# Attention scores of two heads issued in turn, and the expert broadcast, the output stage and the PSUM ring put back to one plain order

## The chip, the cores and the metric

The kernel runs on all 8 cores of one Trainium2 chip. Each core has its own batch entry and all the weights; nothing is exchanged between cores. The metric is the device time in microseconds of the slowest core.

## The reference

For each of 8 batch entries x is 2048 tokens by 1024 features. Attention has 16 heads of 64. The feed-forward part has 8 experts with 4096 hidden features; every token goes to its two best experts, but all experts are computed for all tokens and weighted with `comb`, which is zero elsewhere. Both parts read the same normed input, and both are added to x.

```python
xn = layernorm(x)                        # no scale, no shift
q, k, v = split(xn @ qkv_w.T + qkv_b)    # 16 heads of 64
attn = softmax(q @ k.T / sqrt(64))       # 2048 x 2048 for each head
a = (attn @ v) @ proj_w.T + proj_b
g = xn @ gate_w + gate_b                 # top 2 of 8, softmax over the two
h = gelu(xn @ w1[e] + b1[e])             # for every expert e, 4096 wide
f = sum over e of comb[e] * (h @ w2[e] + b2[e])
out = x + a + f
```

## The kernel before, in words

The program is emitted in one order, and each engine runs its own instructions in that order; a wait at the head of an engine's queue holds all that is behind it. PSUM is four pages `pg0` to `pg3` of 1024 f32 columns, each with two halves of 512. `pread(page, half, token)` notes who read a half last, and `pdeps` makes the next matmul into it wait for that reader. All weights come through two staging buffers `stg` (`stream`, L240): a 512 KB load on the SyncE queue, and a cast to bf16 on VectorE.

**Layernorm** (L290 to L330). 16 tiles of 128 tokens, one after the other: sum on VectorE, mean, squares, variance and root on ScalarE with a reciprocal on VectorE between, the normed tile on VectorE, 8 transposes on TensorE and a copy into `xnT` on ScalarE. Tiles use two sets of small columns and two `xntok` buffers in turn. In the order of emission all steps of a tile stand before those of the next.

**Attention**, for 8 pairs of heads (`hp`; h01 is the head within the pair). `stageA` does two things. `qkv_chunk` makes q and k of both heads, 16 groups of 8 matmuls and a copy on ScalarE each. `p1_chunk` (the max pass) goes over 16 blocks of 128 queries: 8 score matmuls, alternately of the two heads, a row maximum of each on VectorE (L478), then for each head a maximum over four columns (L486), a cast (L491) and a transpose (L502) that puts the negative maximum into row 65 of q, which a copy of 1x1024 on ScalarE places there twice per head. Both draw their PSUM halves from a ring of six, `ASLOTS` (L425).

`stageB` goes over 4 blocks of 512 queries (`qc`), and for each of them first one head, then the other: `p2_chunk` (the score pass of one head) and `av_chunk`. `p2_chunk` issues 16 score matmuls of 512 columns in 8 pairs; a pair fills both halves of one page, and one Exp of 1024 columns on ScalarE reads it. Pages 0 and 1 take turns from pair to pair:

```python
for ktp in range(8):
    page = st["p2n"] % 2
    st["p2n"] += 1
    tks = []
    for j in range(2):
        deps = tmax(aug_tok[b_], attnT_free[h01], pdeps(page, j))
        tks.append(mm(deps, half(page, j)[:, 0:QC], ...))
    ev = act(tks, attnT[h01][...], pg[page][:, :], AF.Exp, scale=1.0 / 8.0)
```

`av_chunk` waits for the last Exp of its head, then makes four groups of 16 small matmuls into page 2 (head 0) or page 3 (head 1), with a reciprocal (L578) and a scaling (L581) on VectorE between two groups of the same page.

**Experts**, 2 token chunks of 1024 by 8 experts, 16 passes. The first half of a pass (the w1 half) is 32 weight blocks x 2 x 8 matmuls of 512 columns with a Gelu on ScalarE each 8; the second (the w2 half) is 8 output blocks `dt` x 2 x 32 matmuls, each 32 followed on VectorE by `ysc` (L797, times the broadcast weight `combbc`) and the addition into `accT` (L802). `cb_emit` (L680) makes `combbc`, two matmuls and two copies on ScalarE; it is called for the next pass after `dt == 2` of this one, into the other of two `combbc` buffers.

**Output.** `emit_final` (L706) is called once after each token chunk, for its 8 tiles: load x into one of three `fxr`, 8 transposes, an addition on VectorE (L723) into one of two `fout`, a store on the GpSimd queue. Its loads wait for the additions into `accT` of their own 512 tokens only.

Of the kernel before, what the change touches and what calls it, by code (L numbers as in the profile page):

```python
# [17 lines left out]
E = 8  # L18
# [11 lines left out]
OPT_A6 = True  # L30
OPT_CB_PRE = True
OPT_FIN_SPLIT = True
OPT_LN2 = True
# [68 lines left out]
def build_program():  # L102
# [48 lines left out]
    cols = nc.alloc_sbuf_tensor("cols", [128, 28], F32)  # L151
# [11 lines left out]
    def at(name, shape, dtype, off):  # L163
# [14 lines left out]
             for i in range(2)]  # L178
# [3 lines left out]
    combbc = [at(f"combbc{i}", [128, 1024], BF16, 90112 + i * 2048)  # L182
              for i in range(2)]
    ysc = [at(f"ysc{i}", [128, 512], BF16, 147456 + i * 1024) for i in range(2)]
    xsq = at("xsq", [128, 1024], F32, 94208)
    xntok = [at(f"xntok{i}", [128, 1024], BF16, 98304 + i * 2048)
             for i in range(2)]
    accT = at("accT", [128, ND * S], BF16, 94208)
    aoutT = at("aoutT", [128, ND * S], BF16, 126976)
    fxr = [at(f"fxr{i}", [128, 1024], F32, 126976 + i * 4096) for i in range(3)]  # L190
    fout = [at(f"fout{i}", [128, 1024], F32, 139264 + i * 4096) for i in range(2)]
# [89 lines left out]
    prev_nm = [None, None]  # L281
    prev_iv = [None, None]
    prev_r = [None, None]
    prev_xn = [None, None]
    prev_tp = [None, None]
    LNC = [(0, 1, 2, 3, 13, 14), (20, 21, 22, 23, 24, 25)]

    xnT_r = xnT[:, :].rearrange("p (d t) -> p d t", d=ND)
    for tt in range(NT):
        pp = (tt % 2) if OPT_LN2 else 0  # L290
        cNS, cNM, cS2, cR, cVA, cIV = (cols[:, j:j + 1] for j in LNC[pp])
        xs = xring[tt % 3]
        xnt = xntok[pp if OPT_LN2 else 0]
        tok_x = dma_in(tmax(xring_free[tt % 3]), xs[:, :],
                       d_x[tt * 128:(tt + 1) * 128, :], sem=f"sX{tt % 3}")
        t_ns = dve(tmax(tok_x, prev_nm[pp]),
                   lambda e, i=xs, o=cNS: e.reduce_sum(o, i[:, :], AX.X,
                                                       negate=True))
        t_nm = act(tmax(t_ns, prev_xn[pp]), cNM, cNS, AF.Identity,
                   scale=1.0 / DM)  # L300
        prev_nm[pp] = t_nm
        t_sq = act([t_nm], xsq[:, :], xs[:, :], AF.Square, bias=cNM,
                   accum=cS2)
        t_va = act(tmax(t_sq, prev_iv[pp], t_consts), cVA, cS2,
                   AF.Identity, scale=1.0 / DM, bias=epscol)
        t_iv = dve(tmax(t_va, prev_r[pp]),
                   lambda e, o=cIV, i=cVA: e.reciprocal(o, i))
        prev_iv[pp] = t_iv
        t_r = act(tmax(t_iv, prev_xn[pp]), cR, cIV, AF.Sqrt)
        prev_r[pp] = t_r  # L310
        t_xn = dve(tmax(t_r, prev_tp[pp]),
                   lambda e, i=xs, o=xnt, m=cNM, r=cR:
                   e.tensor_scalar(o[:, :], i[:, :], m, r, ALU.add, ALU.mult))
        prev_xn[pp] = t_xn
        xring_free[tt % 3] = t_xn
        page = tt % 2
        tp = None
        for dt in range(ND):
            deps = tmax(t_xn, t_id, pdeps(page, 0)) if dt == 0 else []
            tp = tr(deps, pgb[page][:, dt * 128:(dt + 1) * 128],  # L320
                    xnt[:, dt * 128:(dt + 1) * 128], inc=(dt == ND - 1))
        prev_tp[pp] = tp
# [96 lines left out]
    aug_tok = [None] * 4  # L419
    aot_r = [a[:, :].rearrange("p (t c) -> p t c", t=NT) for a in aot]  # L420

    def stageA(hp):
        ring = hp % 2
        chunks = []
        ASLOTS = [(0, 0), (0, 1), (1, 0), (1, 1), (2, 0), (3, 0)]  # L425
        st = {"qk_tok": [], "mq_evs": [[], []], "aqn": 0}

        def qkv_chunk(h01, iq, u, n4):
            def go():
                b_ = 2 * ring + h01  # L430
                buf = qh[b_] if iq == 0 else kh[b_]
                if n4 == 0:
                    st[("w", u)] = stream([wqk_free[u % 3]], wqkbf[u % 3][:, :],
                                          d_wqk[u])
                page, hh = ASLOTS[st["aqn"] % 6]
                st["aqn"] += 1
                deps = tmax(st[("w", u)], ln_all, pdeps(page, hh))
                tk = None
                for dt in range(ND):
                    tk = mm(deps if dt == 0 else [],  # L440
                            half(page, hh)[0:64, :],
                            wqkbf[u % 3][:, dt * 64:(dt + 1) * 64],
                            xnT_r[:, dt, n4 * 512:(n4 + 1) * 512],
                            start=(dt == 0), stop=(dt == ND - 1),
                            inc=(dt == ND - 1))
                ev = act([tk], buf[0:64, n4 * 512:(n4 + 1) * 512],
                         half(page, hh)[0:64, :],
                         AF.Identity, bias=qkvb[:, u:u + 1])
                pread(page, hh, ev)
                st["qk_tok"].append(ev)  # L450
                if n4 == 3:
                    wqk_free[u % 3] = ev
            return go

        for h01 in range(2):
            for iq in range(2):
                u = (2 * hp + h01) + (0 if iq == 0 else 16)
                for n4 in range(4):
                    chunks.append(qkv_chunk(h01, iq, u, n4))

        def p1_chunk(qt):
            def go():
                if qt == 0:
                    st["qk_ready"] = tmax(*st["qk_tok"])
                red_toks = [[], []]
                for kn in range(4):
                    for h01 in range(2):
                        b_ = 2 * ring + h01
                        page, hh = ASLOTS[st["aqn"] % 6]
                        st["aqn"] += 1  # L470
                        deps = tmax(st["qk_ready"], pdeps(page, hh))
                        tk = mm(deps, half(page, hh),
                                qh[b_][0:64, qt * 128:(qt + 1) * 128],
                                kh[b_][0:64, kn * 512:(kn + 1) * 512],
                                start=True, stop=True, inc=True)
                        rd = dve([tk], lambda e, o=mqparts[:, h01 * 4 + kn:
                                                          h01 * 4 + kn + 1],
                                 i=half(page, hh): e.reduce_max(o, i, AX.X))  # L478
                        pread(page, hh, rd)
                        red_toks[h01].append(rd)  # L480
                prev_mb = None
                for h01 in range(2):
                    b_ = 2 * ring + h01
                    c = h01 * 2 + qt % 2
                    t_cb = dve(tmax(prev_mb, *red_toks[h01]),
                               lambda e, s=h01 * 4: e.reduce_max(  # L486
                                   mqnegcol, mqparts[:, s:s + 4], AX.X,
                                   negate=True))
                    t_mb = dve(tmax(t_cb, mqbf_free[c]),
                               lambda e, o=mqbf[:, c:c + 1]:  # L490
                               e.tensor_copy(o, mqnegcol))  # L491
                    prev_mb = t_mb
                    grp = qt // 8
                    pgm = 2 + h01
                    deps = tmax(t_mb, t_id, pdeps(pgm, 1)) if qt % 8 == 0 \
                        else [t_mb]
                    t_tr = b.emit(
                        "tensor", deps,
                        lambda e, o=pgb[pgm][64:65, 1024 + (qt % 8) * 128:
                                             1024 + (qt % 8 + 1) * 128],  # L500
                        i=mqbf[:, c:c + 1]:
                        e.transpose(o, i, ident[:, :], tile_position=(0, 64)),  # L502
                        inc="sMM")
                    mqbf_free[c] = t_tr
                    if qt % 8 == 7:
                        ev = act(tmax(t_tr, aug_free[b_], t_kones[b_]),
                                 qh[b_][64:65, grp * 1024:(grp + 1) * 1024],
                                 pgb[pgm][64:65, 1024:2048], AF.Identity)
                        pread(pgm, 1, ev)
                        st["mq_evs"][h01].append(ev)  # L510
                        if qt == NT - 1:
                            aug_tok[b_] = tmax(*st["mq_evs"][h01])
            return go

        for qt in range(NT):
            chunks.append(p1_chunk(qt))
        return chunks

    def stageB(hp):
# [411 lines left out]
```

How the kernel before makes its waits and increments, by code:

```python
        def op(e, waits=waits, fn=fn, semh=semh, k=k):  # L91
            for (h, v) in waits:
                e.wait_ge(h, v)
            ins = fn(e)
            if semh is not None:
                ins.then_inc(semh, k)
```

## Time and profile before

| | us |
|---|---|
| timed executions, two | 6929.04 and 7074.76 |
| median of the two | 7001.9 |
| profiled execution | 6523.84 |
| span of its slowest core (core 3) | 6522.3 |
| spans of the eight cores | 6481.0 to 6522.3 |
| TensorE busy in the span | 5335.7 (82%) |
| VectorE busy | 1903.5 (29%) |
| ScalarE busy | 1456.3 (22%) |

"Busy" is a share of the whole span, which mixes stages with different limits. The page cuts the span in 40 slices of 163 us and gives for each the busy tenths of every engine and the granted TensorE clock. L219 is the helper `mm`, L225 `tr`, L232 `act`, L212 `cvt`, L208 `dma_in`; so rows of these lines are told apart by their tiles.

### The profile page before, as it was taken

The numbers are of one execution on the slowest core, as the hardware profiler recorded it, in microseconds if no ns is written. First come the engines' busy times: TensorE is split into PE (matmuls) and PEld (weight loads), VectorE is DVE, ScalarE is ACT, GpSimd is POOL, SyncE is SP. The second block draws the span as 40 slices with busy tenths as digits, with TensorE's granted clock in tenths as the row PEclk, the third lists the DMA queues.
The fourth block names the chain that finished last, engine by engine and source line by source line (L and its number), as shares of the span: only waits on it lengthen the run. The fifth ranks groups of instructions, "written<-read, shape, count | busy, mean of one in ns | idle before, by whom it ended". The sixth has DMA issues, their size and how long they took to land.

```text
span 6522.3 us, 68164 instructions; the slowest of 8 cores (6481.0 to 6522.3 us)
## 1 busy us (share of the span) xinstructions
PE 5335.7 (82%) x24976; PEld 2294.2 (35%) x24976; DVE 1903.5 (29%) x3867; ACT 1456.3 (22%) x1942; POOL 8.8 (0%) x20
## 2 busy tenths in 40 slices
PE   2566667666676767999999999998999999999997
PEld 1222223222232323443444444443444444444443
DVE  2334251533515240222222222223222222222222
ACT  3131414223141323220220220220220220220220
POOL 0000000000000000000000000000000000000000
PEclk9656566565655657998999999998999999999998
DMA  2000000000000001443444444444444444443444
GB/s 82 7 1 7 1 7 7 1 7 1 7 3 5 4 1 48 145 148 112 136 147 135 144 148 133 140 153 150 144 144 133 142 149 133 143 147 129 140 156 140
DMA packets 162582, 583.50 MB, mean 89 GB/s; under 512 B 18754, under 2 KB 18882, under 8 KB 162258
## 3 DMA queue, kind: packets, MB, share of 16 engines
q1 hardware_dynamic: 159954, 570.76, 26.7%
q0 software_dynamic: 2304, 8.39, 0.3%
q8 instruction: 207, 3.39, 0.2%
q14 instruction: 117, 0.96, 0.1%
HBM read 570.69 MB, written 8.39 MB: 89 GB/s over the span
## 4 chain that ended last, share of the span: by engine, by line
PE 68%; DMA 12%; DVE 8%; issue 5%; ACT 5%; DVEq 0%; SPq 0%; ACTq 0%; POOL 0%; POOLq 0%
PE pg L219 67%; DMA stg<-w 11%; ACT attnT L232 4%; DVE mqparts L478 3%; DVE w2bf L212 1%; DVE aot L581 1%; DVE mqbf L491 1%; DVE cols L486 1%; DMA y<-fout 1%; DVE w1bf L212 1%; DVE cols L578 1%; PE pg L502 1%; DVEq L93 0%; PE pg L225 0%; DMA stg<-wqk 0%
## 5 line engine op out<-in xcount | busy, mean ns | idle before, releaser
L219 PE MATMUL pg<-xnT,w1bf 128*128 128x512 bf16 x8192 | 1844.4, 389 | 188.6 <-DVE w1bf L212 184.3
L219 PE MATMUL pg<-h_sb,w2bf 128*128 128x512 bf16 x8192 | 1803.7, 383 | 29.1 <-DVE ysc L797 29.1
L232 ACT ACTIVATE h_sb<-pg,b1r_sb 128x512 bf16<-128x512 f32 x1024 | 705.0, 689 | 2432.4 <-PE pg L219 2432.4
L219 PEld LDWEIGHTS pg<-xnT,w1bf 128*128 128x128 bf16 x8192 | 815.7, 100 | 1214.9 <-issue 307.1
L219 PEld LDWEIGHTS pg<-h_sb,w2bf 128*128 128x128 bf16 x8192 | 804.6, 99 | 1024.5 <-issue 128.5
L212 DVE CAST w1bf<-stg 128x1024 bf16<-128x1024 f32 x512 | 355.0, 693 | 1382.8 <-DMA stg<-w 1382.7
L478 DVE TENSOR_REDUCE mqparts<-pg 128x1 f32<-128x512 f32 x1024 | 624.4, 680 | 261.5 <-PE pg L219 260.7
L212 DVE CAST w2bf<-stg 128x1024 bf16<-128x1024 f32 x512 | 355.1, 694 | 991.3 <-DMA stg<-w 991.3
L232 ACT ACTIVATE attnT<-pg 128x1024 bf16<-128x1024 f32 x512 | 498.1, 1023 | 500.3 <-PE pg L219 498.2
L219 PE MATMUL pg<-qh,kh 65*128 65x512 bf16 x1024 | 491.9, 613 | 79.5 <-ACT attnT L232 71.4
L219 PE MATMUL pg<-v_sb,attnT 128*128 128x65 bf16 x4096 | 265.7, 242 | 239.5 <-DVE aot L581 158.5
L219 PE MATMUL pg<-kh,qh 64*128 64x512 bf16 x1024 | 447.4, 612 | 9.2 <-ACT kh L232 7.4
L502 PE MATMUL pg<-ident_sb,mqbf 128*1 128x128 bf16 x256 | 67.7, 265 | 362.9 <-DVE mqbf L491 362.9
L219 PEld LDWEIGHTS pg<-v_sb,attnT 128*128 128x128 bf16 x4096 | 231.7, 129 | 321.0 <-issue 321.0
L797 DVE TENSOR_TENSOR ysc<-pg,combbc 128x512 bf16<-128x512 f32 x256 | 175.9, 687 | 556.1 <-PE pg L219 556.1
L578 DVE RECIPROCAL cols<-pg 128x1 f32<-128x1 f32 x256 | 42.9, 168 | 928.9 <-PE pg L219 928.9
L219 PE MATMUL pg<-xnT,wqkbf 128*64 128x512 bf16 x1024 | 246.7, 406 | 38.2 <-DVE wqkbf L212 35.3
L219 PEld LDWEIGHTS pg<-qh,kh 65*128 65x128 bf16 x1024 | 83.2, 113 | 435.0 <-issue 435.0
L232 ACT ACTIVATE qh<-pg 1x1024 bf16<-1x1024 bf16 x32 | 30.8, 1007 | 854.3 <-PE pg L502 854.3
L219 PEld LDWEIGHTS pg<-kh,qh 64*128 64x128 bf16 x1024 | 127.0, 134 | 239.9 <-issue 218.6
L502 PEld LDWEIGHTS pg<-ident_sb,mqbf 128*1 128x1 bf16 x256 | 20.3, 79 | 494.1 <-issue 494.1
L219 PEld LDWEIGHTS pg<-xnT,wqkbf 128*64 128x64 bf16 x1024 | 118.8, 117 | 164.2 <-issue 70.6
(66 smaller groups left out, 907.8 us busy)
## 6 DMA issues: line engine op xcount, KB each, us to landing
stg<-w SPq DMA_DIRECT2D x1024, 512.0 KB, 3.9
xring<-x SPq DMA_DIRECT2D x16, 512.0 KB, 3.7
stg<-wqk SPq DMA_DIRECT2D x32, 256.0 KB, 2.7
fxr<-x SPq DMA_DIRECT2D x16, 512.0 KB, 5.2
y<-fout POOLq DMA_DIRECT2D x16, 512.0 KB, 6.0
stg<-wv SPq DMA_DIRECT2D x8, 512.0 KB, 5.4
stg<-proj SPq DMA_DIRECT2D x8, 512.0 KB, 4.5
b1r_sb<-b1r SPq DMA_DIRECT2D x1, 128.0 KB
```

The lines of the kernel that those rows point to most:

```text
L212: return b.emit("vector", deps, lambda e, o=out, i=in_: e.tensor_copy(o, i), inc="sDVE")
L219: e.matmul(o, l, r, start=s, stop=t),
L232: e.activation(o, i, f, bias=bi, scale=sc, accum_out=a),
L478: i=half(page, hh): e.reduce_max(o, i, AX.X))
L486: lambda e, s=h01 * 4: e.reduce_max(mqnegcol, mqparts[:, s:s + 4], AX.X, negate=True))
L491: e.tensor_copy(o, mqnegcol))
L502: e.transpose(o, i, ident[:, :], tile_position=(0, 64)),
L578: e.reciprocal(r, i))
L581: e.tensor_scalar(o, i, r, None, ALU.mult))
L797: e.tensor_tensor(o, i, c, ALU.mult))
```

## The change

- Layernorm: one set of small columns and one `xntok` buffer instead of two.
- q and k: the PSUM halves are those of page 0 for q and of page 1 for k, in turn. Max pass: page = head, half = `kn % 2`, that is four halves in the order (0,0), (1,0), (0,1), (1,1), instead of a ring of six.
- Score pass: for each block of 512 queries the matmuls of both heads are issued in turn, head 0 into page 0 and head 1 into page 1; the Exp of a head is issued after its every second matmul. After all 32 of them comes AV of head 0, then AV of head 1. The first matmul waits for `aug_tok` of its own head, as before.
- Experts: one `combbc` buffer. Its two matmuls stand at the head of each pass, and wait for the last addition into `accT` of the pass before.
- Output: all 16 tiles after the last pass. Their loads and their additions wait for `moe_done`, the last of all additions.
- Buffers are placed elsewhere (`ysc`, the output buffers), and four switches and an unused pair of names change.

```diff
-                page, hh = ASLOTS[st["aqn"] % 6]
+                    page, hh = (0 if u < 16 else 1), n4 % 2          # q, k
...
-                        page, hh = ASLOTS[st["aqn"] % 6]
+                    page, hh = h01, kn % 2                           # max pass
...
-                for ktp in range(8):
-                    page = st["p2n"] % 2
-                    st["p2n"] += 1
-                    tks = []
-                    for j in range(2):
-                        kt = 2 * ktp + j
+            for kt in range(16):
+                for h01 in range(2):
+                    b_ = 2 * ring + h01
+                    page, hh = h01, kt % 2
+                    deps = tmax(qk_ready, aug_tok[b_], attnT_free[h01],
+                                pdeps(page, hh))
+                    tk = mm(deps, half(page, hh)[:, 0:QC], ...)
+                    tkp[h01].append(tk)
+                    if kt % 2 == 1:
+                        ev = act(tkp[h01][-2:], attnT[h01][...],
+                                 pg[page][:, :], AF.Exp, scale=1.0 / 8.0)
+                        pread(page, 0, ev)
+                        pread(page, 1, ev)
...
-        for qc in range(NQC):
-            for h01 in range(2):
-                chunks.append(p2_chunk(qc, h01))
-                chunks.append(av_chunk(qc, h01))
...
-        cb_ready = cb_pend.pop(idx, None)
-        if cb_ready is None:
-            cb_ready = cb_emit(idx, ch, e_)
+        for nt in range(2):
+            page, hh = 3, nt
+            deps = tmax(combT_ready, t_sel, combbc_free, pdeps(page, hh))
...
-            if OPT_CB_PRE and nxt is not None and dt == 2:
-                cb_pend[idx + 1] = cb_emit(idx + 1, nxt[0], nxt[1])
-        combbc_free[par] = acc_tok[(ND - 1, ch * 2 + 1)]
-        if OPT_FIN_SPLIT and e_ == E - 1:
-            emit_final(range(ch * 8, ch * 8 + 8))
+        combbc_free = acc_tok[(ND - 1, ch * 2 + 1)]
...
+    for tt in range(NT):
+        tok_x = dma_in(tmax(xr_free[tt % 3], moe_done), xs[:, :], ...)
...
+        t_out = dve(tmax(tk, tok_x, out_free[tt % 2], moe_done), ...)
```

## Rows read from the trace of the kernel before

**Rows 1.** The page, part 2: busy tenths of TensorE in 40 slices, and the granted clock
```profile
PE   2566667666676767999999999998999999999997
PEclk9656566565655657998999999998999999999998
```

**Rows 2.** Groups by line and form: instructions, busy, mean ns, idle time before and its releaser
```profile
L219 PE MATMUL pg<-xnT,w1bf 128*128 128x512 bf16 x8192 | 1844.4, 389 | 188.6 <-DVE w1bf L212 184.3 <-DVE fout L723 4.3
L478 DVE TENSOR_REDUCE mqparts<-pg 128x1 f32<-128x512 f32 x1024 | 624.4, 680 | 261.5 <-PE pg L219 260.7
```

**Rows 3.** Windows, two blocks of the score pass with AV: columns are busy per engine, clock
```profile
760.80:794.05 33.25, 23.28 (x165) 9.69 (x162) 3.61 (x16) 15.53 (x16) 0.00 (x0) 0.50 0.00 1
```

**Rows 4.** Chain of waits in the score pass: start us, us, what
```profile
761.94 1.03 ACT attnT L232
762.97 0.14 issue
763.11 1.02 PE pg L219 x2
...
764.22 1.03 ACT attnT L232
```

**Rows 5.** Timeline, score pass and AV: start us, us, engine, instruction, [idle <-releaser]
```profile
761.94 1.94 ACT L232 ACTIVATE attnT<-pg 128x1024 bf16<-128x1024 f32 x2 [7.68 <-PE pg L219]
...
770.86 1.04 PE L219 MATMUL pg<-v_sb,attnT 128*128 128x65 bf16 x16 [1.27 <-ACT attnT L232]
...
777.60 1.90 PE L219 MATMUL pg<-qh,kh 65*128 65x512 bf16 x4
```

**Rows 6.** Timeline, end of the max pass and start of the score pass
```profile
677.31 1.92 ACT L232 ACTIVATE qh<-pg 1x1024 bf16<-1x1024 bf16 x2 [52.61 <-PE pg L502]
678.58 1.87 PE L219 MATMUL pg<-qh,kh 65*128 65x512 bf16 x4 [0.84 <-ACT qh L232]
679.69 1.94 ACT L232 ACTIVATE attnT<-pg 128x1024 bf16<-128x1024 f32 x2 [0.45 <-PE pg L219]
```

**Rows 7.** Timeline, one block of the max pass
```profile
643.77 3.59 PE L219 MATMUL pg<-kh,qh 64*128 64x512 bf16 x8
644.49 4.87 DVE L478 TENSOR_REDUCE mqparts<-pg 128x1 f32<-128x512 f32 x8 [1.06 <-PE pg L219]
```

**Rows 8.** Timeline, last additions of the last pass, and the output behind them
```profile
6487.16 1.06 PE L225 MATMUL pg<-ident_sb,accT 128*128 128x128 bf16 x16
6488.22 0.43 DVE L802 TENSOR_TENSOR accT<-accT,ysc 128x512 bf16<-128x512 bf16 x1
6488.57 2.35 DVE L723 TENSOR_TENSOR fout<-pg,fxr 128x1024 f32<-128x1024 bf16 x2
6514.40 2.47 DVE L723 TENSOR_TENSOR fout<-pg,fxr 128x1024 f32<-128x1024 bf16 x2 [5.05 <-DMA y<-fout]
```

**Rows 9.** Timeline of TensorE, a border between passes and the output between chunks
```profile
4295.89 100.31 PE L219 MATMUL pg<-xnT,w1bf 128*128 128x512 bf16 x464
4400.04 8.42 PE L219 MATMUL pg<-xnT,w1bf 128*128 128x512 bf16 x32 [3.84 <-DVE w1bf L212]
...
4536.20 1.06 PE L225 MATMUL pg<-ident_sb,accT 128*128 128x128 bf16 x16
...
4564.21 103.18 PE L219 MATMUL pg<-xnT,w1bf 128*128 128x512 bf16 x464 [4.33 <-DVE fout L723]
```

**Rows 10.** Windows: around a 2.39 us idle time, and with the lower clock
```profile
4768.00:4790.00 22.00, 19.61 (x92) 8.77 (x91) 8.11 (x13) 0.00 (x0) 0.00 (x0) 1.00 0.56 177
3010.00:3100.00 90.00, 90.00 (x344) 36.99 (x342) 25.60 (x42) 2.18 (x4) 0.00 (x0) 0.81 0.35 117
```

**Rows 11.** DMA issues of the page: count, KB, median us to landing
```profile
fxr<-x SPq DMA_DIRECT2D x16, 512.0 KB, 5.2
```

**Rows 12.** Timeline of ScalarE in the layernorm, one tile's end and the next's start
```profile
25.64 1.02 ACT L232 ACTIVATE xnT<-pg 128x1024 bf16<-128x1024 bf16 x1 [2.29 <-PE pg L225]
26.56 0.20 ACT L232 ACTIVATE cols<-cols 128x1 f32<-128x1 f32 x1
```

More of the change, by code:

```diff
@@ L418, in build_program @@
     aug_free = [None] * 4
-    aug_tok = [None] * 4
     aot_r = [a[:, :].rearrange("p (t c) -> p t c", t=NT) for a in aot]
-    def stageA(hp):
+    for hp in range(8):
         ring = hp % 2
[L424 to L434, printed above, removed]
-                page, hh = ASLOTS[st["aqn"] % 6]
[L436 to L453, printed above, removed]
@@ L455, in stageA @@
+        qk_tok = []
         for h01 in range(2):
-            for iq in range(2):
-                u = (2 * hp + h01) + (0 if iq == 0 else 16)
+            b_ = 2 * ring + h01
+            h = 2 * hp + h01
+            for (buf, u) in ((qh[b_], h), (kh[b_], 16 + h)):
+                wtok = stream([wqk_free[u % 3]], wqkbf[u % 3][:, :], d_wqk[u])
                 for n4 in range(4):
[L459 to L466, printed above, removed]
-                    for h01 in range(2):
-                        b_ = 2 * ring + h01
-                        page, hh = ASLOTS[st["aqn"] % 6]
[L470 to L481, printed above, removed]
@@ new lines, in build_program @@
+                    page, hh = (0 if u < 16 else 1), n4 % 2
+                    deps = tmax(wtok, ln_all, pdeps(page, hh))
+                    tk = None
+                    for dt in range(ND):
+                        tk = mm(deps if dt == 0 else [],
+                                half(page, hh)[0:64, :],
+                                wqkbf[u % 3][:, dt * 64:(dt + 1) * 64],
+                                xnT_r[:, dt, n4 * 512:(n4 + 1) * 512],
+                                start=(dt == 0), stop=(dt == ND - 1),
+                                inc=(dt == ND - 1))
@@ L482, in go @@
+                    ev = act([tk], buf[0:64, n4 * 512:(n4 + 1) * 512],
+                             half(page, hh)[0:64, :],
+                             AF.Identity, bias=qkvb[:, u:u + 1])
+                    pread(page, hh, ev)
+                    qk_tok.append(ev)
+                wqk_free[u % 3] = qk_tok[-1]
+        qk_ready = tmax(*qk_tok)
+        mq_evs = [[], []]
+        for qt in range(NT):
+            red_toks = [[], []]
+            for kn in range(4):
                 for h01 in range(2):
@@ L492, in go @@
[L492 to L503, printed above, removed]
@@ L513, in p1_chunk @@
[L513 to L519, printed above, removed]
-        ring = hp % 2
-        chunks = []
-        st = {"p2n": 0}
-        def p2_chunk(qc, h01):
-            def go():
-                b_ = 2 * ring + h01
-                exp_toks = []
-                for ktp in range(8):
-                    page = st["p2n"] % 2
-                    st["p2n"] += 1
-                    tks = []
-                    for j in range(2):
-                        kt = 2 * ktp + j
-                        deps = tmax(aug_tok[b_], attnT_free[h01],
-                                    pdeps(page, j))
-                        tks.append(mm(deps,
-                                      half(page, j)[:, 0:QC],
-                                      kh[b_][0:65, kt * 128:(kt + 1) * 128],
-                                      qh[b_][0:65, qc * QC:(qc + 1) * QC],
-                                      start=True, stop=True, inc=True))
-                    aug_free[b_] = tks[-1]
-                    ev = act(tks,
-                             attnT[h01][:, 2 * ktp * QC:(2 * ktp + 2) * QC],
-                             pg[page][:, :], AF.Exp,
-                             scale=1.0 / 8.0)
-                    pread(page, 0, ev)
-                    pread(page, 1, ev)
-                    exp_toks.append(ev)
-                st[("exp", qc, h01)] = tmax(*exp_toks)
-            return go
-        def av_chunk(qc, h01):
-            def go():
-                b_ = 2 * ring + h01
@@ new lines, in build_program @@
+                    page, hh = h01, kn % 2
+                    deps = tmax(qk_ready, pdeps(page, hh))
+                    tk = mm(deps, half(page, hh),
+                            qh[b_][0:64, qt * 128:(qt + 1) * 128],
+                            kh[b_][0:64, kn * 512:(kn + 1) * 512],
+                            start=True, stop=True, inc=True)
+                    rd = dve([tk], lambda e, o=mqparts[:, h01 * 4 + kn:
+                                                      h01 * 4 + kn + 1],
+                             i=half(page, hh): e.reduce_max(o, i, AX.X))
@@ new lines, in build_program @@
+        aug_tok = [None] * 4
+        for h01 in range(2):
+            aug_tok[2 * ring + h01] = tmax(*mq_evs[h01])
+        for qc in range(NQC):
+            exp_toks = [[], []]
+            tkp = [[], []]
+            for kt in range(16):
+                for h01 in range(2):
+                    b_ = 2 * ring + h01
+                    page, hh = h01, kt % 2
+                    deps = tmax(qk_ready, aug_tok[b_], attnT_free[h01],
+                                pdeps(page, hh))
+                    tk = mm(deps,
+                            half(page, hh)[:, 0:QC],
+                            kh[b_][0:65, kt * 128:(kt + 1) * 128],
+                            qh[b_][0:65, qc * QC:(qc + 1) * QC],
+                            start=True, stop=True, inc=True)
+                    aug_free[b_] = tk
+                    tkp[h01].append(tk)
+                    if kt % 2 == 1:
+                        ev = act(tkp[h01][-2:],
+                                 attnT[h01][:, (kt - 1) * QC:(kt + 1) * QC],
+                                 pg[page][:, :], AF.Exp,
+                                 scale=1.0 / 8.0)
+                        pread(page, 0, ev)
+                        pread(page, 1, ev)
+                        exp_toks[h01].append(ev)
+            for h01 in range(2):
@@ L560, in go @@
                     deps = tmax(exp_ready, v_ready, pdeps(page, 0),
-                                aot_free[ring] if (h01 == 0 and qc == 0 and
-                                                   qt == 0) else None)
+                                aot_free[ring] if (h01 == 0 and qc == 0 and qt == 0)
+                                else None)
                     tk = None
@@ L810, in build_program @@
                     [w1_free[ftp % 4]], w1bf[ftp % 4][:, :], d_w1[nxt[1], ftp])
-            if OPT_CB_PRE and nxt is not None and dt == 2:
-                cb_pend[idx + 1] = cb_emit(idx + 1, nxt[0], nxt[1])
-        combbc_free[par] = acc_tok[(ND - 1, ch * 2 + 1)]
-        if OPT_FIN_SPLIT and e_ == E - 1:
-            emit_final(range(ch * 8, ch * 8 + 8))
-    if not OPT_FIN_SPLIT:
-        emit_final(range(NT))
-    moe_done = tmax(*acc_tok.values())
+        combbc_free = acc_tok[(ND - 1, ch * 2 + 1)]
+    moe_done = tmax(*acc_tok.values())
+    out_free = [None, None]
+    xr_free = [None, None, None]
+    last_store = None
+    for tt in range(NT):
+        xs = xring[tt % 3]
+        tok_x = dma_in(tmax(xr_free[tt % 3], moe_done), xs[:, :],
+                       d_x[tt * 128:(tt + 1) * 128, :], sem=f"sX{tt % 3}")
+        page = tt % 2
+        n4g = tt // 4
+        tk = None
+        for dt in range(ND):
+            deps = tmax(acc_tok[(dt, n4g)], pdeps(page, 0)) if dt == 0 \
+                else tmax(acc_tok[(dt, n4g)])
+            tk = tr(deps, pgb[page][:, dt * 128:(dt + 1) * 128],
+                    accT_r[:, dt, tt * 128:(tt + 1) * 128], inc=(dt == ND - 1))
+        t_out = dve(tmax(tk, tok_x, out_free[tt % 2], moe_done),
+                    lambda e, o=outsb[tt % 2][:, :], i=pgb[page][:, 0:1024],
+                    x=xs[:, :]: e.tensor_tensor(o, i, x, ALU.add))
+        pread(page, 0, t_out)
+        xr_free[tt % 3] = t_out
+        t_st = b.emit("gpsimd", [t_out],
+                      lambda e, o=d_y[tt * 128:(tt + 1) * 128, :],
+                      i=outsb[tt % 2][:, :]: e.dma_start(o, i),
+                      inc=f"sOut{tt % 2}", k=16)
+        out_free[tt % 2] = t_st
+        last_store = t_st
     if DBG:
```

235 lines of the change are left out of this document (90 added, 145 removed).

## The prediction

> **What bounds the kernel now.** I read the strip of slices first [rows 1]. It falls into two parts: up to about slice 16 TensorE is busy 5 to 7 tenths with a clock near 0.5 to 0.6, and from there to the end it is busy 9 tenths at 0.9 to 1.0. The expert part is bound by TensorE itself, and only what makes it idle there counts. In the attention part no engine is full, so I looked for a chain. The groups by form [rows 2] show the row maxima of the max pass, 1024 of 680 ns, with little idle time before them: that pass goes at VectorE's pace. A window over two blocks of the score pass with AV [rows 3] shows 15.53 us of ScalarE and 23.28 of TensorE in 33.25 us, at a clock of 0.50, the level of 1.2 GHz. Neither is full, so this pass is bound by a chain of hand-overs, and the chain of waits names it [rows 4]: an Exp of 1.03 us, 0.14 to TensorE, two matmuls in 1.02, 0.06 back to ScalarE, then the next Exp on the same page: 2.28 us from start to start (764.22 - 761.94). In those 2.28 us both pages are served once, since the two chains run side by side: two Exps back to back take 1.94 [rows 5], the second starting 0.92 behind the first.
>
> **Score pass.** This is the main term. The work is the same, 16 matmul pairs and 16 Exps per block of 512 queries; the order is not. After the change the queue of TensorE reads a0 b0 a1 b1 (a is head 0 on page 0, b head 1 on page 1), and the next round a0' b0' a1' b1'. Exp A reads both halves of page 0 and Exp B both of page 1. a0' may start when Exp A ends. b0' stands behind it and needs Exp B, and a1', for which page 0 has long been free, stands behind b0'. Exp A' needs a1'. So the next Exp A waits for Exp B of this round, and the chains that ran side by side become one: Exp A start to Exp B end 1.94 [rows 5], 0.14 to TensorE, b0' and a1' 1.02, 0.06 back [rows 4], together 3.16. By starts it is 2.28 plus the 0.91 by which the pair outlasts one Exp (1.94 - 1.03), 3.19. I take 3.19.
>
> One block of 512 queries for both heads, after:
> - fill a0, b0, a1: four matmuls take 1.90 [rows 5], the last of them 0.63, so three take 1.90 - 0.42 = 1.48, with 0.06 that is 1.54;
> - 7 rounds of 3.19 = 22.33;
> - the last Exp A and its hand-over, 1.03 + 0.14 = 1.17. AV of head 0 needs only this; Exp B runs under it;
> - two AV blocks. The window of 33.25 [rows 3] holds two score passes and two AVs; a score pass lasts 770.86 - 760.80 = 10.06 [rows 3, 5], so the two AVs are 33.25 - 20.12 = 13.13, as they are now.
>
> Sum 38.17, against 33.25 before: +4.92. There are 4 blocks in each of 8 head pairs, 32: **+157.4 us**. The change does save here too: a fill (761.94 - 760.80 = 1.14) and a drain in each block; both are in the sum. Bounds: if a hand-over is 0.1 faster or slower in each of 224 rounds, +/- 22; the lower bound for the whole, that the extra wait costs nothing, is the second rival.
>
> Start of the score pass: before, only head 0's row copy holds the first matmuls, and head 1's runs beside them [rows 6]. Now b0 stands second. The two copies end at 677.31 + 1.92 = 679.23, b0 starts at 679.37, a1 is done at 680.39, and the first Exp starts at 680.45, 1.87 after the first matmul (678.58) where the fill above counts 1.54. +0.33 x 8 = **+2.6 us**.
>
> **Max pass and q, k.** Four halves instead of six. In the rows [rows 7] matmuls follow each other at 0.427 and the maxima at 0.60 (4.87 for 8, the last 0.68 long). With four halves the eighth matmul waits for the fourth maximum: that ends at 644.49 + 3 x 0.60 + 0.68 = 646.97; plus 0.14 and a matmul of 0.63, the result is there at 647.74. VectorE comes to it at 644.49 + 7 x 0.60 = 648.69. There is 0.95 us to spare, and the transposes behind wait for VectorE anyway: **0**. If the cover were gone, a delay of one matmul pitch in each of 128 blocks would be 55 us, the upper bound; below zero nothing is in reach, as VectorE's eight maxima stay. For q and k a group lasts 8 matmuls, over 1.7 us, and a copy with its hand-overs is shorter than that; 0.
>
> The Trainium skill speaks against this zero: its page Perfetto Trace Analysis (Matmul Optimizations) asks that all eight PSUM banks be used, and the change leaves four of them in the max pass. By it the pass would slow down; by the row the 0.95 us decides. The first rival has its price in rows.
>
> **Layernorm.** The second buffers are given up, but the rows show ScalarE going from the copy of one tile straight to the next tile's first step [rows 12], with that tile's sum done by then. In both kernels the copy stands ahead of the next tile in ScalarE's queue; the freed buffers are never waited for. **0**, from both sides: a wait would have to pass that copy, which comes later than all of them.
>
> **Broadcast weights.** The two matmuls per pass stay (moved from `dt == 2`). At the head of a pass they now wait for the last addition of the pass before. In the last pass the next TensorE work, there the transposes, started at 6487.16, right behind the last matmul, and the last addition ended at 6488.22 + 0.43 = 6488.65 [rows 8]; with 0.14 the wait lasts to 6488.79, that is 1.63 us. Now the w1 half starts directly (the one at 4295.89 follows the pass before with no idle time) [rows 9]. 15 borders: **+24.5 us**. What stands behind the waiting matmul is the whole w1 half. Its first four weight blocks are loaded already, and the fifth load waits for the first block's matmuls, so nothing catches up. ScalarE's two copies come before the first Gelu and take less than the first group of matmuls. The clock: the window with an idle time of 2.39 us in the w2 half has it at 1.00 [rows 10], while after 3.84 us a run of 32 matmuls took 8.42 us [rows 9] where 464 at 100.31 give 6.9. 1.63 is below both, so I charge nothing; the bound is 15 such dips of up to 2 us each, 30.
>
> **Output.** Between the chunks TensorE was away from the experts from 4536.20 to 4564.21, 28.0 us, and the 464 matmuls behind it took 103.18 instead of 100.31 [rows 9]: 30.9 us go. At the end, 8 tiles become 16. Loads now wait for the last addition, 6488.65; with 5.2 to landing [rows 11] and 0.1 the first addition stands at 6494.0 instead of 6488.57 [rows 8], +5.4. The tiles go in pairs paced by the stores: (6514.40 - 6488.57) / 3 = 8.6 us per pair here, 8.2 by the pairs between the chunks; four more pairs at 8.4 are 33.6. Together +39.0 - 30.9 = **+8.1 us**; -2 to +25 if pairs take 7.5 or 10.5.
>
> **Sum.** 157.4 + 2.6 + 0 + 0 + 24.5 + 8.1 = **193 us**. Against the profiled execution, 6523.84, that is 6717. The two timed executions took 478 us more than it, 7001.9. The trace has a stretch at a clock of 0.81 in which 342 matmuls took 90 us, 0.263 each [rows 10], against 0.216 (100.31 / 464) at full clock; over the 16384 of the experts that would be 770 us, so timed executions that spend some 60% of the expert part at that level account for it. That is an inference. Attention runs at 0.50 in any case, so my terms add to it rather than scale: **7195 us**.
>
> The Trainium skill (TensorE: Matmul & The Clock Gate, Seeing it yourself) says that a die with three cores in dense matmuls is held at 13/16 while the load lasts. The trace agrees only in the level, 0.81, not in its lasting: here it held for a part of the expert stage.
>
> **The rivals.**
> 1. *The ring of four binds in the max pass.* For it: two halves of PSUM less per head. Against: 0.95 us to spare. Price at most 55 us: 7250. 6 in 100.
> 2. *The extra wait costs nothing* (the other side). Place: b0' behind a0'. Were a1' to reach page 0 in time, a round would stay at 2.28, and a block would be 1.54 + 7 x 2.28 + 1.17 + 13.13 = 31.8, 1.45 less than before: -46 over 32. The sum is -46 + 2.6 + 24.5 + 8.1 = -11: 6991, no change. For it: the pages are swapped at the same rate as now, and TensorE is not full. Against: its queue is in order, and two matmuls plus two hand-overs (1.22) don't fit beside the pair of Exps. It decides where a round is under 2.95: there the sum falls below 140. 9 in 100.
> 3. *Each border between passes throws the clock down.* 15 x up to 2 us on top, 30, and up to twice that if the level stays low longer: about 7240. 8 in 100.
> 4. *The clock rises in the attention part*, as AV of two heads is one longer stretch. At the most all matmul time halves: -0.51 in each of 256 rounds, -0.3 in each of 128 max-pass blocks (the 0.63 of its first matmul), -0.52 in each of 256 AV groups of 1.04, together -302; 6893 is the end of that, and half of it, 7044, what I would expect. Against: AV keeps its pauses for VectorE, and the score rounds get emptier (four matmuls in 3.19 instead of 2.28 us). 4 in 100.
>
> **How the numbers follow.** The forecast itself has 73 in 100, and is 7195 with its own range of 7090 to 7300: +/- 22 for hand-overs, +30 for dips, +17 for the output, and +/- 73 because the two timed executions lie that far from their median. In some 12 of these 73 I expect the timed executions to come near the profiled clock, which would give down to 6717. The range takes in rivals 1, 2 and 3 and leaves out those 12 and part of 4: 6960 to 7320. A difference of 2% (140 us) is about what a measurement can tell from none. The forecast and rivals 1 and 3 are over it: slower 0.86. Rival 2 and most of 4 are within: 0.12. Faster 0.02.
>
> **What would show it.** In the changed profile: a chain Exp, Exp, two matmuls with about 3.2 us from pair to pair of Exps, ScalarE idle some 1.2 before each pair; a block of 512 queries of 38 us; max-pass blocks as long as now; a wait of 1.6 for the addition (L802's successor) at 15 borders, with the clock at 1.00 across it; no gap between the chunks, and about 72 us from the last expert matmul to the end. I am wrong if rounds take under 2.95, or if the clock in the attention part leaves 0.50.

## The result, and the profile after

| | before | after |
|---|---|---|
| timed executions | 10, median of all 6527.58 us | 11, median of all 6772.15 us |
| lowest and highest | 6503.02, 7074.76 | 6698.22, 7357.8 |
| profiled execution | 6523.84 | 6703.29 |
| span of core 3 | 6522.3 | 6697.7 |
| ratio to before | | 1.0304, interval 1.0267 to 1.0342 |

The change makes the kernel 3.0% slower, some 198 us (0.0304 of 6527.58). In part of the executions of either kernel the mean clock of TensorE is lower on one die or on both (0.72 against 0.81 in the longest, 7357.8 us); these are left out of the ratio, and so are the two of before that stood ahead of the prediction, which are of such a length but have no clock on record. Of the ten executions of before known now seven lie between 6503 and 6541.

All rows below from the two main kernels are of core 3, so that they can be laid side by side. First the chain of waits of the kernel after, in the score pass (start us, us, what):

```profile
702.88 0.38 ACT attnT L225
703.26 0.54 issue
703.80 1.03 ACT attnT L225
704.82 0.14 issue
704.96 1.03 PE pg L212 x2
706.02 0.04 issue
706.07 0.38 ACT attnT L225
```

And the timeline of the same place:

```profile
701.77 1.44 PE L212 MATMUL pg<-qh,kh 65*128 65x512 bf16 x3 [0.33 <-ACT attnT L225]
702.88 1.94 ACT L225 ACTIVATE attnT<-pg 128x1024 bf16<-128x1024 f32 x2 [1.25 <-PE pg L212]
704.04 0.59 PE L212 MATMUL pg<-qh,kh 65*128 65x512 bf16 x1 [0.84 <-ACT attnT L225]
704.96 1.44 PE L212 MATMUL pg<-qh,kh 65*128 65x512 bf16 x3 [0.33 <-ACT attnT L225]
706.07 1.94 ACT L225 ACTIVATE attnT<-pg 128x1024 bf16<-128x1024 f32 x2 [1.25 <-PE pg L212]
```

Where the chain of before was one Exp, a hand-over and two matmuls [rows 4], it is now two Exps, the hand-over and two matmuls. The lone matmul at 704.04 is a0', released by Exp A; the next, b0' at 704.96, had to wait for Exp B, and a1' with it. From pair to pair of Exps it is 706.07 - 702.88 = 3.19 us, against 2.28. ScalarE is idle for 1.25 before each pair. The timeline of TensorE a little further on has the first AV group of two blocks, and between them the four matmuls that open the next score pass:

```profile
723.20 1.04 PE L212 MATMUL pg<-v_sb,attnT 128*128 128x65 bf16 x16 [0.84 <-ACT attnT L225]
736.03 1.90 PE L212 MATMUL pg<-qh,kh 65*128 65x512 bf16 x4
761.11 1.04 PE L212 MATMUL pg<-v_sb,attnT 128*128 128x65 bf16 x16 [0.84 <-ACT attnT L225]
```

A block of 512 queries is 761.11 - 723.20 = 37.91 us, where 33.25 stood before [rows 3], and its window (columns as in [rows 3]) shows the clock unchanged at 0.50:

```profile
723.20:761.11 37.91, 24.03 (x160) 10.38 (x161) 3.61 (x16) 15.51 (x17) 0.00 (x0) 0.50 0.00 1
```

Now the border between two passes of the experts, in the timeline of TensorE, and the waits of TensorE summed over the kernel (us, times, longest):

```profile
2990.93 0.59 PE L212 MATMUL pg<-combT,sel_sb 8*128 8x512 bf16 x2 [1.47 <-DVE accT L695]
2991.45 102.01 PE L212 MATMUL pg<-xnT,w1bf 128*128 128x512 bf16 x464
```
```profile
PE pg L212 <- DVE accT L695: 22.1, 15, 1.5
```

The 15 waits for the last addition are there, 1.47 each. But the 464 matmuls behind this one took 102.01, not the 100.31 of before [rows 9]. The windows around it (busy of PE, PEld, DVE, ACT, POOL, then clock, DMA share, GB/s) say why:

```profile
2989.40:2991.00 1.60, 0.13 (x2) 0.10 (x2) 1.33 (x3) 0.00 (x0) 0.00 (x0) 1.00 0.00 0
2991.00:2995.00 4.00, 4.00 (x11) 1.32 (x11) 0.39 (x1) 1.09 (x2) 0.00 (x0) 0.57 0.00 0
2995.00:3000.00 5.00, 5.00 (x25) 2.25 (x23) 0.00 (x0) 2.06 (x3) 0.00 (x0) 1.00 0.30 105
```

The clock fell to the lower level for some 3.4 us right behind the wait (a mean of 0.57 over 4.00 us is 3.4 us at 0.50, and half of them, 1.7, is what 102.01 has over 100.31). I read the length of this run of 464 matmuls at all 15 borders: 102.01 at 12 of them, 100.32 at 3. Core 3 is among the two cores with the most: over the cores 0 to 7 of this execution the longer run comes at 4, 9, 6, 12, 12, 7, 5 and 11 of the 15 borders. In the kernel before, on core 0, it is 100.31 at every border but the one with the output.

Last the end, in the timeline:

```profile
6633.27 1.06 PE L218 MATMUL pg<-ident_sb,accT 128*128 128x128 bf16 x16
6638.81 2.52 DVE L725 TENSOR_TENSOR outsb<-pg,xring 128x1024 f32<-128x1024 bf16 x2 [4.05 <-DMA xring<-x]
6689.79 1.23 DVE L725 TENSOR_TENSOR outsb<-pg,xring 128x1024 f32<-128x1024 bf16 x1 [2.18 <-DMA y<-outsb]
```

From the last expert matmul to the end it is 6697.7 - 6633.27 = 64.4 us, against 35.1 [rows 8].

**Where the 175.4 us between the two spans of core 3 are**, by the starts and ends of the stages (the first row runs from the end of the row copies into q to the copy of the transposed attention output, the second from the first copy of q to the end of the row copies):

| stage | before | after | difference |
|---|---|---|---|
| score pass and AV, mean of 8 head pairs | 133.65 | 153.95 | +20.30, x8 = +162.4 |
| q, k and max pass, mean of 8 | 143.43 | 142.58 | -0.85, x8 = -6.8 |
| all before the experts | 2595.8 | 2750.7 | +154.9 |
| experts, to the last matmul | 3891.4 | 3882.6 | -8.8 |
| end | 35.1 | 64.4 | +29.3 |

The -8.8 of the experts mixes four things: +22.1 of waits, 12 x 1.70 = +20.4 of lower clock, -30.9 for the output that is no longer between the chunks, and the stretch at a clock of 0.81 [rows 10], which the kernel after did not have. Core 0 of before had no such stretch and took 3867.5 for its experts; against it core 3 of the kernel after is +15, and 22.1 + 20.4 - 30.9 is +12. This can't be read to the microsecond: the four cores of before without the stretch took 3849.9 to 3867.5, the eight of after 3856.8 to 3884.2.

### The profile page after: what moved, and what is told of

Its sections match the earlier page's. It is cut to its first block, busy times and chain, and to the rows that moved or that the text cites. A ratio compares the mean times of both kernels' runs of the same rounds, so it can differ in the third digit from the quotient of the medians.

```text
span 6701.6 us, 68218 instructions; the slowest of 8 cores (6667.0 to 6701.6 us)
## 1 busy us (share of the span) xinstructions
PE 5384.7 (80%) x24976; PEld 2289.6 (34%) x24976; DVE 1904.3 (28%) x3867; ACT 1452.6 (22%) x1942; POOL 8.8 (0%) x20
## 4 chain that ended last, share of the span: by engine, by line
PE 62%; DMA 13%; DVE 9%; issue 9%; ACT 6%; DVEq 0%; SPq 0%; ACTq 0%; POOL 0%; POOLq 0%
PE pg L212 61%; DMA stg<-w 11%; ACT attnT L225 5%; DVE mqparts L452 3%; DVE w2bf L205 1%; DVE aot L536 1%; DVE mqbf L463 1%; DMA y<-outsb 1%; DVE cols L460 1%; DVE cols L533 1%; PE pg L473 1%; DVE w1bf L205 1%; DVE ysc L690 0%; DVEq L89 0%; PE pg L218 0%
## 5 line engine op out<-in xcount | busy, mean ns | idle before, releaser
L212 PE MATMUL pg<-h_sb,w2bf 128*128 128x512 bf16 x8192 | 1784.1, 380 | 36.6 <-DVE ysc L690 36.4
L212 PE MATMUL pg<-qh,kh 65*128 65x512 bf16 x1024 | 514.8, 611 | 272.4 <-ACT attnT L225 263.3
L212 PE MATMUL pg<-kh,qh 64*128 64x512 bf16 x1024 | 488.2, 595 | 18.8 <-DVE mqparts L452 7.8
L225 ACT ACTIVATE combbc<-pg 128x512 bf16<-128x512 f32 x32 | 17.4, 594 | 1724.9 <-PE pg L212 1724.9
L212 PEld LDWEIGHTS pg<-qh,kh 65*128 65x128 bf16 x1024 | 103.6, 117 | 657.6 <-issue 657.6
L212 PEld LDWEIGHTS pg<-kh,qh 64*128 64x128 bf16 x1024 | 104.4, 112 | 360.4 <-issue 341.0
```

The source lines that it names most:

```text
L212: e.matmul(o, l, r, start=s, stop=t),
L225: e.activation(o, i, f, bias=bi, scale=sc, accum_out=a),
```

## The experiments

Each starts from the kernel before unless it says otherwise. "Theory" is the chain of the prediction.

**The scores in turn, alone.**

```diff
-        chunks.append(p2_chunk(qc, h01)); chunks.append(av_chunk(qc, h01))   # per head
+        for kt, h01 in [(2*r + j, h01) for r in range(8) for j in range(2) for h01 in range(2)]:
+            page, hh = h01, kt % 2      # a0 b0 a1 b1, Exp at each second kt
+        ...                             # then AV of head 0, AV of head 1
```

> The kernel before with one part of the change alone: in the score pass the matmuls of both heads are issued in turn (a0 b0 a1 b1), then AV of head 0, then AV of head 1. The theory of the chain (Exp A of the next round waits for Exp B of this one) expects rounds of 3.19 us, a block of 512 queries about 37.9 us instead of 33.0, and 150 to 165 us more in all: a ratio near 1.024. The rival, that the added time of the whole change sits in the borders between passes and the output, expects less than 40 us more.

Ratio 1.0224, interval 1.0135 to 1.0313. In its trace a head pair's score pass with AV takes 154.15 us on the mean of eight (133.65 before), the same as in the changed kernel, so +164 us. The interval alone leaves 88 to 204 us; that is already over the rival's 40, and the trace puts it at 164. This one part carries nearly the whole change; the rival is out.

**The scores in pairs.** The same, with the two innermost loops exchanged: a0 a1 b0 b1.

```diff
-        for kt, h01 in [(2*r + j, h01) for r in range(8) for j in range(2) for h01 in range(2)]:
+        for kt, h01 in [(2*r + j, h01) for r in range(8) for h01 in range(2) for j in range(2)]:
```

> As the run before, but the matmuls come in pairs of one head (a0 a1 b0 b1); both AVs still stand behind both score passes. The theory of the chain expects that only the order of issue costs: rounds go back to 2.28 us, a block is 1.14 + 7 x 2.28 + 1.17 + 13.13 = 31.4 us, and the kernel is 50 to 60 us faster than before (about 0.991). The rival, that the loss comes from doing two heads at once with AV behind both (fewer places where AV and Exp overlap), expects it 100 us or more slower, as the run before.

Its timeline, ScalarE and TensorE:

```profile
678.58 1.94 ACT L232 ACTIVATE attnT<-pg 128x1024 bf16<-128x1024 f32 x2 [0.34 <-PE pg L219]
679.75 1.93 PE L219 MATMUL pg<-qh,kh 65*128 65x512 bf16 x4 [0.35 <-ACT attnT L232]
680.86 1.94 ACT L232 ACTIVATE attnT<-pg 128x1024 bf16<-128x1024 f32 x2 [0.34 <-PE pg L219]
```

A round is 680.86 - 678.58 = 2.28 again, and the head pair takes 126.25 us, 7.4 less than before, 59 us in all: the expected 50 to 60. Only four executions were timed, too few for a ratio; the lowest is 6450.56 and the spans of the profiled one are 6434.9 to 6449.0. Two heads at once cost nothing; exchanging two matmuls in TensorE's queue costs 0.91 us a round.

**The same exchange in the changed kernel.**

```diff
-            for kt in range(16):
-                for h01 in range(2):
+            for ktp in range(8):
+                for h01, kt in ((0, 2*ktp), (0, 2*ktp+1), (1, 2*ktp), (1, 2*ktp+1)):
```

> The changed kernel with one thing put back: the score matmuls in pairs of one head (a0 a1 b0 b1). The theory of the chain expects 0.91 x 7 + 0.4 = 6.8 us less in each of 32 blocks, 210 to 220 us less than the changed kernel, about 6490: faster than the kernel before, by 0.5%. The rival, that other parts of the change cost as much as the order of issue, expects it to stay slower than the kernel before by over 1%.

Ratio to before 0.9947, interval 0.9924 to 0.997, lowest 6468.62; the head pair takes 126.06. Against 1.0304 for the changed kernel that is 3.6%, some 230 us (223 by the head pairs, 8 x 27.9), from the order of four instructions. With this alone put back, the rest of the change does not even lose: the 59 us that the common score pass of two heads gives in pairs more than cover the waits at the borders.

**The broadcast at the head, alone.**

```diff
-OPT_CB_PRE = True
+OPT_CB_PRE = False
-        par = idx2 % 2          # and par = idx % 2
+        par = 0                 # one buffer
```

> The kernel before with the broadcast weights made at the head of each pass into one buffer, alone. The theory expects 15 waits of about 1.5 us for the last addition, 22 to 25 us more, and the clock untouched by them. The rival, that each wait throws the clock down, expects 50 us or more.

Ratio 1.0042, interval 1.0009 to 1.0075, that is 27 us (6 to 49). Its waits on core 5:

```profile
PE pg L219 <- DVE accT L802: 20.6, 14, 1.5
```

The fifteenth, behind the output between the chunks, is covered there. The run of 464 matmuls behind the border took 102.01 at 10 of 14 borders on core 5 and at 8 of 14 on core 0, so 14 to 17 us of lower clock come on top of 20.6. Theory and rival were both half right: the wait and the fall of the clock are both real, and together they are 34 to 38 us by the trace, within the interval of the ratio, whose upper end of 49 us is under the rival's 50. (The trace's own executions are single ones.)

**The output at the end, alone.**

```diff
-OPT_FIN_SPLIT = True
+OPT_FIN_SPLIT = False
-            slab = tmax(*(acc_tok[(dt, n4g)] for dt in range(ND)))
+            slab = tmax(*acc_tok.values())     # loads and additions wait for all
```

> The kernel before with all 16 output tiles after the last pass, their loads and additions waiting for all additions into accT, alone. The theory: 28 us between the chunks and 3 us of lower clock behind them go, and the end grows by 29 us as in the changed kernel: between -6 and +8 us. The rival, that the end is paced as in the kernel before (8.4 us per pair of tiles), expects +8 us; that the loads fight the stores, +25 us.

Ratio 0.9982, interval 0.9946 to 1.0017: no difference that can be told, and at most 11 us more. On core 3 its end takes 6521.6 - 6453.9 = 67.7 us, 32.6 more than before, against 30.9 saved in the middle:

```profile
6454.99 0.42 DVE L802 TENSOR_TENSOR accT<-accT,ysc 128x512 bf16<-128x512 bf16 x1
6458.92 2.49 DVE L723 TENSOR_TENSOR fout<-pg,fxr 128x1024 f32<-128x1024 bf16 x2 [3.51 <-DMA fxr<-x]
...
6513.75 2.46 DVE L723 TENSOR_TENSOR fout<-pg,fxr 128x1024 f32<-128x1024 bf16 x2 [2.36 <-DMA y<-fout]
```

Seven steps from pair to pair in 54.8 us are 7.8 each, where I had taken 8.4. The rival of 25 us is out.

**The ring of four, alone**, twice, since the first time gave too few executions for a ratio (lowest 6501.2).

```diff
-                page, hh = ASLOTS[st["aqn"] % 6]      # q, k
+                page, hh = (0 if u < 16 else 1), n4 % 2
-                        page, hh = ASLOTS[st["aqn"] % 6]      # max pass
+                        page, hh = h01, kn % 2
```

> The kernel before with the halves of q, k and the max pass of the changed kernel (four in place of a ring of six), alone. The theory: 0.95 us to spare in each block of the max pass, nothing lost; the traces even show 0.9 us less per head pair, so -7 to 0 us. The rival, that four halves bind, expects up to +55 us.

> The same kernel as s5 again, for an interval: the max pass took 110.7 us per head pair there, 110.6 before. The theory (0.95 us to spare) expects a ratio of 1.000 within 0.003; the rival (four halves bind) up to 1.008.

Ratio 0.9996, interval 0.9969 to 1.0024. Two blocks of the max pass in the second one's timeline:

```profile
645.14 3.93 PE L219 MATMUL pg<-kh,qh 64*128 64x512 bf16 x8
645.86 4.88 DVE L476 TENSOR_REDUCE mqparts<-pg 128x1 f32<-128x512 f32 x8 [1.06 <-PE pg L219]
...
651.93 3.93 PE L219 MATMUL pg<-kh,qh 64*128 64x512 bf16 x8
```

The eight matmuls take 3.93 instead of 3.59 [rows 7], so the last ones do wait for a half, as worked out (a result at 3.97 behind the first start), and the eight maxima take 4.88 instead of 4.87: the slack swallows it. A block is 651.93 - 645.14 = 6.79 us.

**The layernorm with one buffer, alone.**

```diff
-OPT_LN2 = True
+OPT_LN2 = False
```

> The kernel before with one set of columns and one xntok buffer in the layernorm, alone. The theory: ScalarE's order already serializes the tiles, 0 us; first copy into xnT at 25.6 and last at 111.7 us as before. A rival, that the freed buffer is waited for, expects 16 x 1 us or more in the first 130 us.

Ratio 0.9986, interval 0.9958 to 1.0015. The copies into xnT start from 26.0 to 112.1 us, against 25.6 to 111.7: the same 86.1 from first to last. What was not looked for is in the same trace: the max pass of a head pair, from the start of the last copy of q and k to the end of the row copies, takes 110.2 us on cores 0, 3 and 5, where the kernel before takes 110.6 to 110.7. In the kernel before two of the 16 blocks of every max pass are 0.2 to 0.4 us longer than the usual 6.78 (the same ones on all three cores); here, as in the changed kernel, none is.

**Pairs, and the AV groups of the two heads in turn**, an attempt to beat both kernels, twice.

```diff
-            for h01 in range(2):
-                chunks.append(av_chunk(qc, h01))
+            for qt in range(QC // 128):
+                for h01 in range(2):
+                    chunks.append(av_chunk(qc, h01, (qt,)))   # rzcol by (2 * gq + h01) % 4
```

> The score pass in pairs (a0 a1 b0 b1) and, behind it, the AV groups of the two heads in turn, so that VectorE's work on page 2 lies under the matmuls on page 3. The theory of hand-overs expects two groups each 1.85 us where one took 1.85: AV of both heads 7.3 us instead of 13.1, 5.8 x 32 = 186 us less than with pairs alone, about 6260 us. The rival, that TensorE's own matmuls and weight loads fill the time (16 matmuls of 65 columns in 1.04), expects at most half of that, over 6350.

> The same kernel as s7 again, for an interval: the theory of hand-overs, with the higher clock that s7's trace shows in the AV part (1.00 for stretches where the kernel before has 0.50), expects 0.95 to 0.96 of the kernel before. If s7's 6213 us was one lucky execution, it comes nearer the 0.963 that the hand-overs alone give.

The first has a lowest time of 6213.46 and spans up to 6211.8; the second a ratio of 0.9516, interval 0.946 to 0.9572. That is 4.8% faster than before and 7.6% faster than the changed kernel (0.9516 / 1.0304 = 0.9235). The timeline of the first, core 5:

```profile
710.23 6.19 PE L219 MATMUL pg<-v_sb,attnT 128*128 128x65 bf16 x112 [0.46 <-ACT attnT L232]
716.70 0.66 PE L219 MATMUL pg<-v_sb,attnT 128*128 128x65 bf16 x16 [0.28 <-DVE cols L579]
...
717.19 1.03 PE L219 MATMUL pg<-qh,kh 65*128 65x512 bf16 x4
```

Seven AV groups run without a pause, and both heads' AV takes 717.19 - 710.23 = 6.96 us where it took 13.1. The head pair takes 97.86. That is 28.4 less than with pairs alone, 227 us in all, more than the 186 expected. Against the run with pairs alone, both on core 5, the 32 AVs of both heads give 200 (421.6 us become 222.0), 14 more than expected, and the 32 score passes give 24 (584.8 become 560.6). These 24 are clock: the four score matmuls behind AV take 1.03 us instead of 1.90 [rows 5], and the windows over one block, over the middle of its score pass and behind its AV are

```profile
693.16:717.19 24.03, 19.71 (x167) 8.66 (x163) 3.34 (x16) 15.36 (x16) 0.00 (x0) 0.64 0.01 2
700.00:709.00 9.00, 7.61 (x17) 1.09 (x16) 0.00 (x0) 7.66 (x9) 0.00 (x0) 0.50 0.00 0
717.00:719.00 2.00, 1.22 (x16) 0.48 (x12) 0.74 (x3) 1.12 (x2) 0.00 (x0) 1.00 0.02 4
```

0.64 over the block, 0.50 in the latter part of its scores, 1.00 behind AV: the level of 2.4 GHz comes with the dense AV, near its end, and is lost again in the score rounds. With pairs alone, where AV has its pauses, the clock is 0.50 through the whole stretch from 680 to 800 us of core 5.

**The kernel of the last experiment, with the output at the end and early loads of x.**

```diff
-OPT_FIN_SPLIT = True
+OPT_FIN_SPLIT = False
-            tok_x = dma_in(tmax(fin_state["xfree"][sx], slab), ...)
+            tok_x = dma_in(tmax(fin_state["xfree"][sx], proj_done), ...)
```

> s7 with all output tiles at the end and their x loads free to start when the buffers are (not waiting for the additions). Expected from the rows: 31 us between the chunks go, the end grows by 29 to 33, and the early loads save about 5: 0 to 8 us less than s7. A rival, that the loads of x now compete with the weight loads of the last pass, expects no gain or a few us more.

Ratio 0.9562, interval 0.9517 to 0.9607: no better than without it, the intervals overlap. The gain of up to 8 us is not to be seen.

## Why the prediction was right or wrong

The stated time, 7195 us with a range of 6960 to 7320, was wrong: 6772 is the median, outside it. The difference that the change makes was right: 193 us forecast, 3.04% or 198 us measured, 179 between the two profiled executions; and so was the chain behind its main term. That the sum comes out so close is in part luck, as shown below.

**The step that failed** is the last of the sum, the choice of what to add it to. The prediction had 6717 for the profiled execution's own clock and then took the median of the two timed executions as the base, giving 12 in 100 to the other. The base of 7001.9 was wrong by 476 us: the eight executions of before that were timed later have a median of 6526, seven of them within 6503 to 6541, and only one, 7004.41, is near the two. The changed kernel's profiled execution took 6703.29, 14 from 6717. Two timed executions that lie 478 us above a profiled one, and 146 us from each other, were a warning that they were not typical. The mistake was not the inference about their cause, which no run here contradicts, but to take them for the rule; what I should have done is to let the range reach down to 6717.

Point by point:

- **Score pass, +157.4, and its start, +2.6.** Right. The round is 3.19 as worked out, the block 37.91 (38.17), the head pair +20.30 (20.0): +162. The run with the scores in turn alone shows the same in its trace, and the exchange of two matmuls takes it away in either kernel. Rival 2 is out.
- **Max pass, q and k, 0.** Right; the last of the eight matmuls ends 3.93 behind the first start (3.97 worked out), and the slack holds. Rival 1 is out. The changed kernel is even 0.85 us per head pair faster up to the score pass, 7 us in all. The ring of four alone doesn't show it (110.7 for the max pass, 110.6 before, 110.06 after); the changed kernel with pairs does (110.2), and so does the kernel before with one layernorm buffer (110.2). So most of the gain in the max pass comes with the layernorm's part of the change, for which the prediction charged nothing; how one layernorm buffer shortens blocks of the max pass stays open.
- **Layernorm, 0.** Right for the layernorm itself (86.1 us from first to last copy, before and with one buffer).
- **Broadcast, +24.5.** The wait was right (22.1), the clock wrong. I had argued from an idle time of 2.39 us that left the clock at 1.00 [rows 10] that 1.5 us could not lower it. It did, at 12 of 15 borders on core 3, for 1.70 us each: 20 us on top, inside the 30 that bounded it; on core 0, with 4 borders, 7 us. Rival 3 was true in its mechanism, and in its price to a quarter (core 0) to two thirds (core 3). One row in which a longer pause had done no harm was no proof, and the same trace of before, core 3, has one that speaks against it, an idle time of 2.48 us in a w2 half with the lower level behind it:

```profile
5982.21 8.11 PE L219 MATMUL pg<-h_sb,w2bf 128*128 128x512 bf16 x29 [2.48 <-DVE ysc L797]
```
```profile
5983.00:5987.00 4.00, 4.00 (x13) 1.48 (x11) 1.83 (x4) 0.00 (x0) 0.00 (x0) 0.57 0.39 134
```

- **Output, +8.1.** Close: -30.9 + 29.3 = -1.6. The first addition came 5.5 behind the first transpose (6638.81 - 6633.27), where 6494.0 - 6487.16 = 6.8 was worked out, and the pairs went at some 7.3 instead of 8.4. The stated lower end of -2 doesn't follow from its own condition: 8 pairs at 7.5 instead of 8.4 give +0.9. Nor do the 72 us named as a sign: 35.1 + 39.0 is 74; it was 64.4.
- **Sum.** On core 3 it is 162 - 7 + 22 + 20 - 2 = 195, against 193: the clock at the borders made up for what the max pass and the output did better. That is luck: with the 7 us that the clock took on core 0 the same sum would be 182 (the two spans of core 0 lie 191 apart, since its end grew by 36).
- **Rival 4**, a rising clock in the attention part, did not come with AV of two heads behind one another, which keeps its pauses. It did come once the pauses were taken away.

## What to carry to other kernels

When two chains share an in-order queue, write down the order of their instructions and ask of each what it waits for: the chains run side by side only as long as no instruction of one stands between two of the other that must both be done before the next step. Here a0 a1 b0 b1 and a0 b0 a1 b1 issue the same work and differ by 0.91 us in every round of 2.28. Where two groups take turns on two pages, let them do so group by group, and the other engine's share lies under the matmuls. And before adding a difference to a time, see whether the timed and the profiled executions agree; if not, both belong in the range.

## What was not expected of the hardware

Behind a wait of 1.47 us the granted clock of TensorE was at the lower level for some 3.4 us at 4 to 12 of 15 places, depending on the core. In the w2 halves of before the length of the idle time alone doesn't decide either. On core 3 idle times of 2.04, 2.23, 2.25 and 2.39 us left the clock at 1.00 and one of 2.48 did not; on core 0 those of 2.20 and 2.43 left it and those of 2.01, 2.33 and 2.44 did not. Of the 20 between 1.0 and 1.9 us on these two cores none lowered it, while those of 1.47 at the borders did. What tells the cases apart was not tried. In the other direction, the clock rose from 0.50 to 1.00 near the end of the dense AV of the best version, which gave some 24 us in the score passes beside what the removed pauses gave.
